# First batch's self-attention inside the set-up of a decoder layer, with the weights' grid values in bf16

## What is computed

```python
x = x + _L0_attn_ref(_layernorm(x, axis=-1))
x = x + _L0_xattn_ref(_layernorm(x, axis=-1), ctx_512, Wq, Wkv_expand, Wout)
x = x + _L0_ffn_ref(_layernorm(x, axis=-1), w_gate, w_up, w_down)

def _quantize_elem(x, ebits, mfrac, max_norm):     # on blocks divided by their scale
    ax = jnp.abs(x)
    priv = jnp.floor(jnp.log2(jnp.where(ax == 0, 1.0, ax)))
    min_exp = float(-2 ** (ebits - 1) + 2)
    priv = jnp.maximum(priv, min_exp)
    scale = jnp.exp2(priv - mfrac)
    q = jnp.round(x / scale) * scale
    return jnp.clip(q, -max_norm, max_norm)
def _q_w(w):
    return _quantize_mx(w, 2, 1.0, 2.0, 6.0)
```

## Time and profile before

| | us |
|---|---|
| median of 3 runs | 1676.1 |
| lowest and highest | 1673.59, 1677.09 |
| the profiled execution's own time | 1672.65 |
| its span, first to last instruction | 1670.9 |
| PE, DVE, ACT, POOL busy, share of the span | 83%, 69%, 51%, 33% |
| set-up, up to the barrier | 0 to 136 |
| first self-attention and head | 136 to 190 |

### The profile page before, as it was taken

One profiled execution on the slowest core, in us unless ns is written; L12 is line 12 of the kernel. 1 busy time (PEld: TensorE's weight loads), 2 busy tenths in 40 slices (PEclk: granted clock), 3 DMA queues, 4 the chain that ended last, 5 costly groups with the idle time before them and its releaser, 6 DMA issues.

```text
span 1670.9 us, 31184 instructions
## 1 busy us (share of the span) xinstructions
PE 1385.5 (83%) x11267; PEld 802.3 (48%) x11344; DVE 1147.6 (69%) x2475; ACT 854.8 (51%) x2098; POOL 547.2 (33%) x494
## 2 busy tenths in 40 slices
PE   1224899879988899889988899889988899889987
PEld 0113564445544555445544565445544564445533
DVE  8994456975578556975578556965588556965576
ACT  2542464456634564456635564456635564456622
POOL 6882001650046101650046101650046101650055
PEclk9999999999999999989999999989999999989999
DMA  5311000000010000000000001000010000000001
GB/s 196 112 57 39 1 2 26 7 14 14 2 27 14 20 1 27 7 18 10 2 26 14 20 1 26 7 20 7 2 26 14 20 2 26 7 20 2 2 0 26
DMA packets 25285, 36.07 MB, mean 22 GB/s; under 512 B 2480, under 2 KB 10672, under 8 KB 25136
## 3 DMA queue, kind: packets, MB, share of 16 engines
q1 hardware_dynamic: 25136, 34.09, 7.6%
HBM read 25.69 MB, written 8.39 MB: 20 GB/s over the span
## 4 chain that ended last, share of the span: by engine, by line
PE 41%; DVE 31%; ACT 11%; issue 6%; POOL 2%; DMA 0%; SPq 0%; ACTq 0%; POOLq 0%; DVEq 0%
PE psum L1101 9%; PE psum L1118 8%; PE psum L529 7%; DVE top L810 6%; PE psum L1139 4%; DVE inter L836 4%; PE psum L1155 4%; DVE q L806 3%; PE psum L1104 3%; ACT p L955 3%; DVE nmx L760 2%; ACT silu L993 2%; DVE top L813 2%; DVE x_f L511 2%; DVE tmp L585 2%
## 5 line engine op out<-in xcount | busy, mean ns | idle before, releaser
L760 DVE TENSOR_REDUCE nmx<-psum 128x2 f32<-128x1024 f32 (+3 forms) x256 | 210.7, 823 | 167.3 <-PE psum L1104 166.6
L506 POOL TENSOR_TENSOR rstd<-var_eps,minus_half 128x1 f32<-128x1 f32 x96 | 58.2, 610 | 795.3 <-DVE var_eps L500 795.1
L955 ACT ACTIVATE p<-psum,nmx 128x384 f32<-128x384 f32 (+3 forms) x512 | 266.2, 527 | 63.8 <-DVE nmx L760 42.8
L1118 PE MATMUL psum<-ident,p 128*128 128x128 f32 x1280 | 204.8, 281 | 12.7 <-ACT pt L979 6.9
L773 DVE COPY pt<-psum 128x512 f32<-128x512 f32 (+3 forms) x256 | 124.7, 487 | 129.1 <-PE psum L1118 127.5
L1101 PE MATMUL psum<-k_f,q_f 32*128 32x512 f32 (+3 forms) x1024 | 206.8, 480 | 5.8 <-ACT p L955 5.3
L1201 PE MATMUL psum<-wd_sb,iq_t 128*128 128x512 bf16 x483 | 147.9, 425 | 74.3 <-ACT iq_t L1001 44.6
L694 POOL TENSOR_TENSOR inter<-inter,rscale 128x512 f32<-128x512 f32 x128 | 140.1, 1094 | 184.9 <-DVE rscale L844 183.1
L1118 PEld LDWEIGHTS psum<-ident,p 128*128 128x128 f32 x1280 | 138.7, 140 | 53.6 <-issue 19.0
L979 ACT COPY pt<-psum 128x512 f32<-128x512 f32 (+3 forms) x256 | 109.3, 427 | 97.7 <-PE psum L1118 95.5
L694 POOL TENSOR_TENSOR iq<-q,scale 128x512 bf16<-128x512 fp8e4 x128 | 143.7, 1123 | 8.7 <-DVE q L806 8.7
(11 more groups left out here) (104 smaller groups left out, 2436.0 us busy)
## 6 DMA issues: line engine op xcount, KB each, us to landing
x_in<-in_x_dram SPq DMA_DIRECT2D x32, 256.0 KB, 4.0
out_dram<-x_res SPq DMA_DIRECT2D x64, 128.0 KB, 2.4
w_raw<-in_w_gate_dram SPq DMA_DIRECT2D x16, 256.0 KB, 2.7
w_raw<-in_w_up_dram SPq DMA_DIRECT2D x16, 256.0 KB, 3.0
w_raw<-in_w_down_dram SPq DMA_DIRECT2D x16, 256.0 KB, 3.6
ctx_in<-in_ctx_t_dram SPq DMA_DIRECT2D x8, 256.0 KB, 2.9
wq_raw<-in_wq_t_dram SPq DMA_DIRECT2D x1, 1024.0 KB, 8.3
wo_sb<-in_wo_t_dram SPq DMA_DIRECT2D x1, 1024.0 KB, 10.0
```

The source lines that it names most:

```text
L760: dve.tensor_reduce(nmx2[:, u % UNITS, 2 * pr:2 * pr + 2], where(("scores2", oc, qt, pr))[:, :, 0:(qt + 1) * P], AX_X, ALU.max, negate=Tru ...
L955: ins = act.activation(p2[:, (4 * u + hh) % P2_RING, 0:m], where(label)[:, hh % 2, 0:m], ACT.Exp, bias=nmx2[:, u % UNITS, hh:hh + 1], accu ...
L1118: last = pe.transpose(where(label)[:, 0, kt * P:(kt + 1) * P], p2[:, (4 * u + hh) % P2_RING, kt * P:(kt + 1) * P], ident[:])
```

## The change

The first batch's self-attention moves from the second block into the set-up. It gets the bank "C1" for itself; the turned weights, which alternated between banks 6 and 7, get bank 6 alone. Its loads are issued after the first three steps' weights and ahead of `wq` and `wo`. DVE's part i = j - 1 follows step j (from j = 3), POOL's too (from j = 2); PE's products of a part come ahead of the step's transposes, ACT's behind the step's magic. The low part of `wkv` is made in step 2, that of the context in step 1. `wq_raw` lies in `x_res`; the scales keep 4 slots and not 16; `w_clip` gives way to an f32 `w_sum` and a `w_grid` in bf16, which the rounding writes and the clip changes in place. In the second block only the head is left of the first batch's steps.

```diff
+SCALES = 4
+def first_step(j):
+    t, part = divmod(j, 4)
+    return ([("xT1", t)], [("scores1", t, 0), ("scores1", t, 1)], [("v", t)], [("out1", t)])[part]
-            plan[("T", "C1")[turn[0] % 2]].append(label)
+            plan[("T", "C1")[turn[0] % 2] if b else "C1"].append(label)
+            ("w_sum", [P, 3, D], F32), ("w_grid", [P, 2, 3, D], BF16), ("w_q", [P, 2, 3, D], BF16),
-        def turned_of(n):
-            return psum[:, 6 + n % 2, 0:256].bitcast(BF16)
+        def turned_of():
+            return psum[:, 6, 0:256].bitcast(BF16)
...
+            def _(sp):
+                for j in range(RAW):
+                    load_weights(sp, j)
+                load_x(sp, 0, 0)
+                sp.dma_start(ctx_in[:], ctx_t[0]).then_inc(ctx_loaded, 16)
+                sp.dma_start(wkv_raw[:], wkv_t).then_inc(wkv_loaded, 16)
+                load_x(sp, 0, 1)
+                sp.dma_start(wq_raw[:], wq_t.rearrange("(c p) n -> p c n", p=P)).then_inc(wq_loaded, 16)
+                sp.dma_start(wo_sb[:], wo_t.rearrange("(c p) n -> p c n", p=P)).then_inc(wo_loaded, 16)
...
+            def _(pool):
+                scaled_rows(0)
+                scaled_rows(1)
+                attend_pool(pool, 0, 0)
+                for j in range(STEPS):
+                    scaled_back(j)
+                    if j + 2 < STEPS:
+                        scaled_rows(j + 2)
+                    if j >= 2:
+                        attend_pool(pool, 0, j - 1)
+                attend_pool(pool, 0, 4 * T - 1)
+                attend_pool(pool, 0, 4 * T)
...
+            def _(dve):
+                for j in range(STEPS):
+                    if later:
+                        top_done = block_maxima(j + 2)
+                    dve.wait_ge(wmagic_ready, j + 1)
+                    sum_done = count(dve.scalar_tensor_tensor(out=total, in0=magic, scalar=W_ROUND, in1=y,
+                                                              op0=ALU.add, op1=ALU.add))
+                    if j == 0:
+                        attend_vector(dve, link, 0, 0)
+                    if later:
+                        top_done = powers(j + 2, top_done)
+                    dve.wait_ge(w_chain, sum_done)
+                    if j >= 2:
+                        dve.wait_ge(wq_ready, j - 1)
+                    rounded_done = count(dve.scalar_tensor_tensor(out=grid, in0=magic, scalar=W_ROUND, in1=total,
+                                                                  op0=ALU.add, op1=ALU.subtract, reverse1=True))
+                    if later:
+                        top_done = scale(j + 2, top_done)
+                    dve.wait_ge(w_chain, rounded_done)
+                    dve.tensor_scalar(grid, grid, W_MAX, -W_MAX, ALU.min, ALU.max).then_inc(wclip_ready, 1)
+                    if j + 1 < STEPS:
+                        exponents(j + 1)
+                    if later:
+                        inverse(j + 2, top_done)
+                    if j == 0:
+                        attend_vector(dve, link, 0, 1)
+                    if j == 1:
+                        low_ctx(dve, 0)
+                    if j == 2:
+                        dve.wait_ge(w_high, 1)
+                        dve.tensor_tensor(wkv_hl[:, 1], wkv_raw[:], wkv_hl[:, 0].bitcast(F32),
+                                          ALU.subtract).then_inc(wkv_ready, 1)
+                    if j >= 3:
+                        attend_vector(dve, link, 0, j - 1)
+                attend_vector(dve, link, 0, 4 * T - 1)
+                dve.wait_ge(w_high, 2)
+                dve.tensor_tensor(wq_hl[:, 1], wq_raw[:], wq_hl[:, 0].bitcast(F32), ALU.subtract).then_inc(consts_done, 1)
+                attend_vector(dve, link, 0, 4 * T)
+                attend_vector(dve, link, 0, 4 * T + 1)
...
+            def _(pe):
+                for j in range(STEPS):
+                    for label in first_step(j):
+                        if label == ("v", 0):
+                            pe.wait_ge(wkv_ready, 1)
+                        attend_product(pe, label)
+                    pe.wait_ge(wq_ready, j + 1)
+                    for m in range(3):
+                        if 3 * j + m:
+                            pe.wait_ge(w_stored, 3 * j + m)
...
+            def _(act):
+                for j in range(STEPS):
+                    if j + 1 < STEPS:
+                        magic(j + 1)
+                    if j == 0:
+                        high_ctx(act, 0)
+                    if j % 4 == 0:
+                        take_xt1(act, j // 4)
+                    if j % 4 == 1:
+                        exps1(act, j // 4)
+                    if j % 4 == 2:
+                        take_v(act, j // 4)
+                    if j % 4 == 3 and j > 4:
+                        normalise2(act, j // 4 - 1)
...
+                normalise2(act, T - 1)
+        nc.all_engine_barrier()
```

More of the change, by code:

```diff
@@ L595, in attend_vector, with high_ctx, take_xt1, exps1 @@
                 shift2_of(dve, g - 1)
+        def high_ctx(act, b):
+            act.wait_ge(ctx_loaded, 16 * (b + 1))
+            if b:
+                until_filled(act, ("k", b * OC - 1))
+            act.copy(ctx_hl[:, 0, :], ctx_in[:]).then_inc(S["ctx_high"], 1)
+        def take_xt1(act, g):
+            label = ("xT1", g)
+            until_filled(act, label)
+            if g >= 2:
+                until_filled(act, ("scores1", g - 2, 1))
+            free(act.copy(x_t[:, g % 2, :], where(label)[:, 0, :]), label)
+        def exps1(act, g):
+            for r in range(2):
+                label = ("scores1", g, r)
+                until_filled(act, label)
+                if g >= 2:
+                    until_filled(act, ("out1", g - 2))
+                free(act.activation(e1[:, g % 2, r, :], where(label)[:, 0, 0:C * HALF], ACT.Exp,
+                                    bias=self_shift[:], scale=SCALE), label)
+        def take_v(act, g):
+            label = ("v", g)
+            until_filled(act, label)
+            free(act.copy(v_sb[:, g % T, :], where(label)[:, 0, :]), label)
         def attend_scalar(act, b, i):
@@ L613, in attend_scalar @@
-            if part == 1 and 0 <= t < T:
-                for r in range(2):
-                    label = ("scores1", g, r)
-                    until_filled(act, label)
-                    if g >= 2:
-                        until_filled(act, ("out1", g - 2))
-                    free(act.activation(e1[:, t % 2, r, :], where(label)[:, 0, 0:C * HALF], ACT.Exp,
-                                        bias=self_shift[:], scale=SCALE), label)
+                take_xt1(act, g)
+            if part == 1 and 0 <= t < T:
+                exps1(act, g)
@@ new lines, in _ @@
+            @block.tensor
+            def _(pe):
[3 more added lines that the diff above has]
+                            pe.wait_ge(wkv_ready, 1)
+                        attend_product(pe, label)
+                    pe.wait_ge(wq_ready, j + 1)
+                    for m in range(3):
+                        if 3 * j + m:
+                            pe.wait_ge(w_stored, 3 * j + m)
+                        for c in range(4):
+                            last = pe.transpose(turned_of()[:, c * P:(c + 1) * P],
+                                                w_q[:, j % 2, m, c * P:(c + 1) * P], ident_b[:])
+                        last.then_inc(w_turned, 1)
@@ L673, in _ @@
+        nc.all_engine_barrier()
+        with nc.Block() as block:
+            @block.sync
+            def _(sp):
                 for b in range(B):
@@ L718, in scale_back @@
                     by_scales(iq[:, i % RING, :], q8[:, i % RING, :], scale6[:, i % RING, :], "iq_ready")
-                for i in range(P1_STEPS):
-                    attend_pool(pool, 0, i)
                 for b in range(B):
@@ L863, in head @@
                         low_xt2(b * T + 3)
-                for i in range(P1_STEPS):
-                    attend_vector(dve, link, 0, i)
+                for i in range(4 * T, P1_STEPS):
                     head(0, i)
@@ L1010, in head @@
                         take_q(b * OC)
-                for i in range(P1_STEPS):
-                    attend_scalar(act, 0, i)
+                for i in range(4 * T, P1_STEPS):
                     head(0, i)
@@ L1214, in head @@
                         project_q(b * OC)
-                for i in range(P1_STEPS):
-                    attend_tensor(pe, 0, i)
+                for i in range(4 * T, P1_STEPS):
                     head(0, i)
```

349 lines of the change are left out of this document (143 added, 206 removed).

## The result

| | before | changed |
|---|---|---|
| median | 1675.55 (4 runs, 1673.59 to 1677.09) | 1662.33 (4 runs, 1661.74 to 1663.66) |
| ratio, 95% interval | 1 | 0.9919 [0.9907, 0.9930] |
| the profiled execution's own time | 1672.65 | 1662.52 |
| its span | 1670.9 | 1660.7 |
| clip 0 to clip 15 | 108.8 | 140.4 |

The medians differ by 13.2 us. 1661 had been forecast from a gain of 15.2. A clip with a number is the clip of that set-up step, and a period is the time from one clip's start to the next.

The account below looks back on a forecast made before the run. DVE was taken to bound the set-up. Removing 45.1 us, less 28.7 for longer periods and 1.2 at the end, gave 15.2 less: 1657.5 against the profiled execution, 1661 as median, range 1650 to 1673.

Parts of the forecast that it names:

- What goes: The first batch's self-attention alone behind the barrier, 136.37 to 181.5: 45.1 us removed; the head behind it stays at 8.2.
- a slow PE: In the head, PE coming out of the thinly used set-up might run slower: up to 3.5 us more.
- The clip: DVE's clip in bf16, each set-up step: clip to exponents 0.87 becomes 0.49, a gain of 0.38 between 0 and 0.72.
- The waits for POOL: In the set-up, nine moved DVE instructions each wait 2.36 us for POOL's product to end, 21 us in all.
- The periods: Fifteen set-up periods, clip 0 to clip 15, grow from 109.2 to 137.9 with DVE's added work: 28.7 us longer.
- The failed term: the loads: Loads moved ahead of step 3's weights, arriving some 4 us later: costed at nothing, without cover a wait up to 4, once.
- The end: From clip 15 to leaving the set-up's barrier: 10.2 us where it was 9.0, so 1.2 more.
- The sum: Whole kernel: 45.1 - 28.7 - 1.2 = 15.2 us less, 1657.5 against the profiled execution, median 1661.
- No waits for POOL: Rival, 8%: the nine set-up instructions run beside POOL without waiting, 21 us come back: 1640.
- The small prices: Rival, 18%: the clip gains nothing (5.7) and PE is slow through the head (3.5): 1667 to 1670.
- POOL keeps its turn: Rival, 8%: DVE waits for both POOL products, each of nine waits growing by 2.77: 25 us, 1686.
- The ring of PE and ACT: Rival, 6%: their series through one bank makes magic late in most set-up steps; at 0.5 a step 1669.

Follow-up runs that it names:

- e10: The changed kernel repeated unaltered, a third profile; the execution's own time 1660.59 us.
- e5: The changed kernel with the grid values back in f32, the self-attention left in the set-up; 1668.87 us, ratio 0.9958.
- e6: The kernel before with the bf16 grid alone, the self-attention left behind the barrier; 1669.90 us, ratio 0.9964.
- e3: The changed kernel with its nine waiting DVE instructions put ahead of the step's clip, not behind the reciprocal; 1644.83 us, ratio 0.9816.
- e2: The changed kernel with the first batch's shifts written with one tensor source and a scalar per partition; 1654.81 us, ratio 0.9878.
- e1: The changed kernel with loads of wkv, x's second half, wq and wo issued behind the weights of steps 3 to 6; 1658.93 us, ratio 0.9902.
- e8: e4 plus POOL's rows of step 1 waiting for DVE's first exponents, and wq's subtraction moved behind the barrier; 1637.84 us, ratio 0.9774.
- e7: The changed kernel with one extra ACT copy of the third turned tile in each step; 1662.03 us, ratio 0.9918.
- e9: The changed kernel repeated unaltered, a second profile; the execution's own time 1662.79 us.
- e4: The changed kernel with both the nine DVE instructions ahead of the clip and the later loads; 1641.29 us, ratio 0.9797.

## Why the prediction was right, step by step

*What goes.* The 45.1 us between barrier and head went as said, and the head, taken at 8.2, measured 8.1. Little of the 3.5 set as a bound for a slow PE came: the k projection did run at v's pace (1.63 for three products, 1.33 before), and the early fourth tile paid for it. The query products took 3.12 in the first profile; in e10 they took 3.49, and the head 8.6.

*The clip.* Middle of the bounds 0.38, measured 0.40 in each period (e5, e6). The 0.38 was a choice between two bounds and not derived, so that it came this close is luck. The estimate from the Trainium skill (VectorE: DVE Perf Modes, Mode 4×_2P), 0.4 and a fixed part, agrees with the trace: the clip takes 0.56.

*The waits for POOL.* Forecast 2.36 for each and the work left behind it, so 2.7 for normalise, 2.4 for the shift, 3.0 and 3.4 for the two subtractions; measured 2.63, 2.44, 2.90 and 3.43. That they are waits for POOL's product is shown by e3, where the same instructions last 0.54 and 0.15 once POOL has done. That the second SBUF tensor makes the shift wait is shown by e2. Normalise has one tensor and two scalars per partition, and e2's shift had such a scalar and didn't wait; no run here tells what in normalise makes it wait. The rule of the Trainium skill (SBUF — State Buffer, Who interferes with whom) puts it down to a two-port mode. The trace agrees with that rule in the instructions that don't wait as well: moments and sums, with one source, kept their 0.65 and 0.67 beside POOL.

*The periods.* Forecast 8.0, 11.4, 9.3, 6.6, 7.7, and 9.8 and 10.3 for steps 1 and 2; measured 7.90, 11.46, 9.23, 6.63, 7.60, 9.76 and 10.29.

*The failed term: the loads.* Costed at nothing, with the words "some 4 us later" and step 0's growth of 3.5 as cover. The data came 8.6 us later than before (28.3 for 19.7), and the first period was 13.7 and not 9.6. The estimate took the old rate, 314 GB/s, for the new mix of transfers; the rate was 246, and SP's own issue stood for 3.42. Why the rate fell and the issue took so long, no run shows. The prediction named the price without that cover, "a wait of up to 4, once": 4.14 was it. e1 gives it back.

*The end.* Forecast 10.2 from clip 15 to the barrier's exit, measured 10.1. The subtraction for wq did wait for POOL, then POOL's addition for it (3.31 for 1.26, where e8 moved the subtraction away), as laid out.

*The sum.* With 15.2 forecast, the end of the first query projection should have come 15.2 earlier; it came 11.4 earlier. Of that difference of 3.8 the loads explain 4.1, so the rest of the sum held to 0.3. Of the 11.4 the first profile shows 9.9 at the second batch, since the first batch took 185.4 and not 183.9 us; the prediction had left all of that stretch as it was. The forecast median is 1.3 off, nearer than the working deserves: the sum promised 4 too much, since it left the wait for the loads out, and the profile of the kernel before, on which it was made, ran 3 us under its median. The medians' gain of 13.2 lies between; that it comes closer to the 15.2 than the profiles' 11.4 does is luck as far as the working goes (the last section has a possible reason, which is not shown).

*The rivals.* No waits for POOL: out, by the durations. The small prices: out, since the clip gave its 0.40 and the head took 8.1. POOL keeps its turn: out, since each of the nine waiting instructions ended behind one POOL product, in eight of them with the next one queued (65.87, beside 65.55). The ring of PE and ACT: out, by e7 and by e3's periods of 6.88.

## What to carry to other kernels

Work put into another engine's idle time isn't placed by dependencies alone: on DVE beside POOL, the shift and the subtractions with their two SBUF tensors, and normalise too, cost the rest of POOL's instruction, here 2.3 us for an operation on one column. Put such instructions where POOL has finished (e3: 17.5 us for the same work), or write them with one tensor and a scalar per partition (e2). When transfers are brought forward, price those that they overtake: here a wait of 4 us for weights stood behind data that could come later at no cost (e1).

## What the runs showed that was not expected

A race decides the start. DVE's first exponents and POOL's second product come free within 0.2 us of one another, and whichever starts first makes the other wait: 0.90 and 0.96 or 3.51 for the exponents, clip 0 at 20 or at 23, in profiles of the same program (first profile and e9 against e10). With one wait in POOL's stream the exponents came first and took 0.90 (e8, one profile).

The kernel before has the same race. Its first exponents, and those of e6, which leaves this part of it as it was:

```profile
11.13 0.90 DVE L379 TENSOR_SCALAR w_pow<-w_y 128x1536 int32<-128x1536 int32 x1
```

```profile
11.75 3.51 DVE L379 TENSOR_SCALAR w_pow<-w_y 128x1536 int32<-128x1536 int32 x1 [0.30 <-POOL w_y L328]
```

Clip 0 is at 18.56 in the first and at 21.80 in the second, and no wait for loads levels it out: e6's periods are the same 6.88 from the first on. So the profile on which the forecast was made had the early start. If most executions of the kernel before start late, that is the 3 us by which this profile ran under its median; no run shows how often each start comes.

The stretch of the first batch, in which nothing was changed, took 183.9 us in the profile of before and 185.4, 185.1 and 184.1 in three of the changed kernel. The granted clock of that stretch, in the busy time by stretch (columns as in the earlier trace rows), of before and of the first profile after:

```profile
189.80:373.60 183.80, 163.80 (x1361) 93.26 (x1369) 126.49 (x291) 99.85 (x254) 55.71 (x56) 0.97 0.04 11
```

```profile
178.40:363.70 185.30, 165.41 (x1360) 93.32 (x1369) 126.47 (x291) 99.77 (x254) 55.72 (x56) 0.96 0.05 11
```

PE is granted 2.4 GHz in that stretch but for two or three pieces of 3 to 7 us at half, 1.2 GHz. The first of them begins at 317.9 in the profile of before, and at 263.5, 307.5 and 302.0 in the three after, so their places differ between executions of one program. The stretch's length goes with them: where the first fall comes 85 us behind the first query projection (first profile, e3, e5) it is 185.3 to 185.8, where it comes 124 us behind it (e1, e2, e7, e10) 184.1 each time, and 130 us behind it (e4, e8, e9) 184.8 to 185.1. But the two profiles without the move, before and e6, have 183.9 and 183.7, under all ten with it. What sets the falls, how much of the 1.5 us they account for, and whether the move adds a little to this stretch, stays open.
